# Expert tiles of 256 slots, with the inner layer turned and the first weight's parts fetched per tile

## The chip, the core and the metric

The kernel runs on one core of one Trainium2 chip. The metric is the device time of one execution in microseconds. The engines are named as in the profile: PE (matmul), PEld (its weight loads), DVE, ACT, POOL, SP, and 16 DMA engines that all queues share.

## What is computed

A graph network of two layers over 12,500 nodes and 200,000 edges is followed by a mixture of experts, to which the change belongs:

```python
logits = jnp.einsum('bsd,de->bse', xn, Wr) + br
top_vals, top_idx = jax.lax.top_k(logits, K)          # K = 2 of E = 8
w = jax.nn.softmax(top_vals, axis=-1)
...
for e in range(E):
    h = jax.nn.gelu(jnp.einsum('bsd,dh->bsh', xn, W1[e]) + b1[e], approximate=False)
    y_e = jnp.einsum('bsh,hd->bsd', h, W2[e]) + b2[e]
    y = y + y_e * w_full[..., e, None]
```

A row has D = 256 channels, the hidden layer H = 512, and the output 256. Everything is float32.

## The kernel before

The stages run one after the other with a barrier between them: the graph layers (`project_input`, `sum_layer`, `normalize_sums`, `project_hidden`, then the sums again), `route_tokens`, `list_tiles` and `run_experts`. The change is in the last two, and in `project_hidden`.

**project_hidden** takes the nodes in 24 chunks of 512 (and a last one of 256), two at a time. ACT normalizes (L1091), PE multiplies (L1111), DVE adds the bias (L1129), POOL takes the maximum with 0 (L1145), and SP stores 512 KB for each chunk (L1073). A buffer of `h` is written again only when its store from two chunks before has landed.

**route_tokens** writes one list of slots for each expert into the DRAM table `table`. Each entry has a token's row number and its weight. **list_tiles** counts the tiles of each expert on DVE, with one small step after the other, while SP loads all weights: `ffn_w1` and `ffn_w2` (4 MB each) and the biases, spread over all partitions.

**run_experts** goes over `FFN_TILES` = 204 tiles of 128 slots; a tile belongs to one expert, and a tile that no slot needs is run on dummy rows. First ACT and DVE split both weights into a high and a low part (16 pairs of instructions on 128x1024), since each product is made of three float32r products: high by high, high by low, low by high. For tile s the work is:

- POOL gathers its 128 rows from `tokens` (L1736, into one of `ROWS_HELD` = 6 places), 5 tiles ahead
- PE turns them (L1772, 2 transposes); ACT scales them by gamma and beta (L1854); DVE splits them (L1913, L1915)
- PE, first product: 6 matmuls of 512 columns (L1786); DVE adds b1 (L1906); ACT does gelu (L1860)
- PE turns the hidden rows (L1795, 4 transposes); ACT takes the high part (L1866), DVE the low one (L1922)
- PE, second product: 12 matmuls of 256 columns (L1804); DVE adds b2 (L1946); ACT weighs them by the slot's weight (L1885)
- POOL scatters the 128 result rows into `out`, adding to what is there (L1755)

The order on each engine is written out by hand, and every engine works through its own queue in order. PE's step s is: turn the rows of s+3, first product of s+2, turn the hidden rows of s+1, second product of s. POOL's step s is: gather s+5, then scatter s. SP loads the table (L1714) and holds back a scatter (L1725) until all scatters of the expert before have landed (`tile_after`), as two experts may add to one row. Tiles past the last used one all write to the same dummy rows, so each of them waits until the one before has landed.

## Time and profile before

| | |
|---|---|
| median of three runs | 5430.35 us (5423.59 to 5431.04) |
| the profiled execution | 5421.78 us |
| its span, first to last instruction | 5420.2 us |
| PE busy in the span | 4191.7 us (77%) |
| DVE busy | 3213.5 us (59%) |
| POOL busy | 3789.6 us (70%) |
| ACT busy | 966.8 us (18%) |
| DMA moved | 560.35 MB, mean 103 GB/s |

The span's busy shares are means over stages that have different limits. The graph sums fill most of the span and are not touched. `project_hidden` is a stretch of 103 us at 2155, and `run_experts` runs from 4580 us to the end, some 840 us. The profiled execution is 8.6 us shorter than the median of the runs.

### The profile page before, as it was taken

What the parts mean: (1) busy time and instruction counts of PE and PEld (TensorE: products, weight loads), DVE (VectorE), ACT (ScalarE), POOL (GpSimd) and SP (SyncE); (2) the same over time, 40 slices, a digit from 0 to 9 for tenths busy, and PEclk for the clock granted to TensorE, in tenths of its full rate; (3) what the DMA queues carried; (4) which work ended last, traced back from release to release, by engine and by line L of the source; (5) the groups of instructions that cost most, each with busy time, mean ns of one, the idle gap of its engine ahead of it and who ended that gap; (6) DMA issues with size and microseconds to landing.
All of it is one profiled execution on the core that took longest, in us unless ns stands there. A gap on an engine that the chain in (4) does not pass through costs nothing. (4 is left out here: it accounts for less than half of the span.)

```text
span 5420.2 us, 135489 instructions
## 1 busy us (share of the span) xinstructions
PE 4191.7 (77%) x20451; PEld 3507.4 (65%) x20452; DVE 3213.5 (59%) x9144; ACT 966.8 (18%) x2131; POOL 3789.6 (70%) x3818
## 2 busy tenths in 40 slices
PE   6778787778777874877878787777776672999998
PEld 5566666666666663766666666666665672888886
DVE  6555555555555556555555555555655664666665
ACT  3100000000000003200000000000001652566665
...
DMA packets 359801, 560.35 MB, mean 103 GB/s; under 512 B 128849, under 2 KB 253393, under 8 KB 359474
## 3 DMA queue, kind: packets, MB, share of 16 engines
...
q14 instruction: 48, 0.39, 0.0%
HBM read 479.80 MB, written 79.41 MB: 103 GB/s over the span
## 5 line engine op out<-in xcount | busy, mean ns | idle before, releaser
L788 POOL DMA_INDIRECT c_messages<-h,c_indices x3038 | 2879.9, 948 | 950.6 <-issue 918.3
L824 PE MATMUL c_partial<-c_onehot,c_messages 128*128 128x128 f32 x12544 | 2759.7, 371 | 851.2 <-DMA c_messages<-h,c_indices 448.0
L824 PEld LDWEIGHTS c_partial<-c_onehot,c_messages 128*128 128x128 f32 x12544 | 2263.1, 260 | 1350.4 <-issue 775.8
L867 DVE TENSOR_TENSOR sums<-sums,c_partial 128x256 f32 x3136 | 1321.0, 421 | 1590.0 <-PE c_partial L824 1531.5
L840 DVE TENSOR_SCALAR c_onehot<-iota,edge_dst,edge_w 128x128 f32<-128x128 f32 x3152 | 1148.2, 365 | 14.4 <-PEq L103 14.3
L750 ACT ACTIVATE c_indices<-edge_src 128x16 int32 (+1 forms) x200 | 42.9, 215 | 3706.6 <-PE c_partial L824 2752.9
L1755 POOL DMA_INDIRECT out<-ffn_result,ffn_table x204 | 326.4, 1600 | 213.9 <-ACT ffn_result L1885 127.4
L1736 POOL DMA_INDIRECT ffn_rows<-tokens,ffn_table x209 | 215.7, 1032 | 71.5 <-issue 57.2
L804 PE MATMUL c_z<-sums,w 128*128 x768 | 260.6, 501 | 0.0
L1398 POOL DMA_INDIRECT table<-rt_entry,rt_slot x196 | 203.8, 1040 | 69.2 <-issue 57.9
L1804 PE MATMUL ffn_ps<-ffn_w_high,ffn_hT_high 128*128 x816 | 246.9, 303 | 0.0
L1804 PE MATMUL ffn_ps<-ffn_w_high,ffn_hT_low 128*128 x816 | 229.6, 281 | 0.0
L1804 PE MATMUL ffn_ps<-ffn_w,ffn_hT_high 128*128 x816 | 229.5, 281 | 0.0
L804 PEld LDWEIGHTS c_z<-sums,w 128*128 128x128 f32 x768 | 198.4, 272 | 35.1
L1854 ACT ACTIVATE ffn_xT<-ffn_ps_x,beta,gamma 128x128 f32<-128x128 f32 x416 | 167.6, 453 | 178.6 <-PE ffn_ps_x L1772 177.1
L1913 DVE CAST ffn_xT_high<-ffn_xT 128x256 fp32r<-128x256 f32 x207 | 73.3, 354 | 192.6 <-ACT ffn_xT L1854 156.0
L1786 PE MATMUL ffn_ps<-ffn_w_high,ffn_xT_high 128*128 x412 | 183.8, 446 | 0.3 <-DVE ffn_xT_low L1915 0.3
L1922 DVE TENSOR_TENSOR ffn_hT_low<-ffn_ps_h,ffn_hT_high 128x512 fp32r<-128x512 f32 x205 | 141.7, 691 | 43.2 <-ACT ffn_hT_high L1866 39.5
L1786 PE MATMUL ffn_ps<-ffn_w_high,ffn_xT_low 128*128 x412 | 164.9, 400 | 0.0
L1786 PE MATMUL ffn_ps<-ffn_w,ffn_xT_high 128*128 x412 | 164.1, 398 | 0.0
L1772 PE MATMUL ffn_ps_x<-ident,ffn_rows 128*128 128x128 f32 x416 | 87.8, 293 | 89.4 <-DMA ffn_rows<-tokens,ffn_table 70.8
L1804 PEld LDWEIGHTS ffn_ps<-ffn_w,ffn_hT_high 128*128 128x128 f32 x816 | 154.7, 190 | 0.0
...
## 6 DMA issues: line engine op xcount, KB each, us to landing
...
```

What stands on the lines that cost most here:

```text
L788: pool.indirect_dma_start(messages[:, k, :], None, source, bass.IndirectOffsetOnAxis(ap=indices[:, k:k + 1], axis=0)).then_inc(s_message[k ...
L804: last = pe.matmul(z[:, co, :], t["w2"][:, k, co * P:(co + 1) * P], sums[:, k, bass.ds(chunk * Z_COLS, Z_COLS)], start=(k == 0), stop=(k = ...
L824: last = pe.matmul(partial[:, k % TURN_BANKS, g * P:(g + 1) * P], messages[:, k, g * P:(g + 1) * P], onehot[:, k % TURN_ONEHOTS, :], start ...
L840: return dve.tensor_scalar(onehot[:, slot, :], t["iota"][:], t["edge_dst"][:, bass.ds(step, 1)], t["edge_w"][:, bass.ds(step, 1)], ALU.is_ ...
L867: dve.tensor_tensor(where, where, partial[:, k % TURN_BANKS, 0:C].rearrange("p (g n) -> p g n", g=CG), ALU.add).then_inc(s_added, 1)
L1398: pool.indirect_dma_start(d["table"], bass.IndirectOffsetOnAxis(ap=slot[:, b, c, j:j + 1], axis=0), entry[:, b, c, j, :], None).then_inc(s ...
L1736: pool.indirect_dma_start(rows[:, row_slot, :], None, d["tokens"], bass.IndirectOffsetOnAxis(ap=table[:, k, 0:1], axis=0)).then_inc(s_rows ...
L1755: pool.indirect_dma_start(d["out"], bass.IndirectOffsetOnAxis(ap=table[:, k, 0:1], axis=0), result[:, k % 2, :], None, compute_op=ALU.add) ...
L1786: last = pe.matmul(ps_1[:, q, :], rows_part[:, q, g, :], w_part[:, bass.ds(e * (CG * HIDDEN) + g * HIDDEN, HIDDEN)], start=(g == 0 and n = ...
L1804: last = pe.matmul(ps_2[:, q, 0:C], rows_part[:, q, g * P:(g + 1) * P], w_part[:, bass.ds(e * (HG * C) + g * C, C)], start=(g == 0 and n = ...
L1854: act.activation(xT[:, q, g, :], ps_x[:, g * P:(g + 1) * P], ACT.Identity, bias=t["beta"][:, g:g + 1], scale=t["gamma"][:, g:g + 1]).then_ ...
L1922: dve.tensor_tensor(hT_low[:, q, :], ps_h[:, q, :], hT_high[:, q, :].bitcast(F32), ALU.subtract).then_inc(s_hT_low, 1)
```

## The change

- A tile has 256 slots (`TILE`), in two halves of 128, and there are (25088 + 8 * 255) // 256 = 105 tiles. POOL issues two gathers and two scatters for a tile, since each takes 128 rows.
- The first product is computed turned: the weight's 128x128 blocks are the stationary side and the 256 turned rows are the moving one, so that its result has the hidden channels on the partitions. It is now 24 matmuls of 256 columns. The transposes of the hidden rows are gone, b1 becomes a per-partition bias of gelu on ACT (from `b1T`), and both ACT steps write into PSUM in place. DVE takes both parts, in two halves of 128x512.
- The parts of the first weight don't stay on chip. `project_hidden` makes them, one expert with each of the first 8 pairs of chunks: it loads 512 KB, splits them on ACT and DVE, and stores 1 MB to the DRAM tensor `w1_parts`. `run_experts` fetches the 1 MB of the tile's expert for each tile on SP's queue (`load_parts`), into two buffers.
- `list_tiles` loads neither `ffn_w1` nor the spread b1; the split of 16 pieces at the start of `run_experts` is one of 8.
- The order by hand is a new one. PE's step s is: turn the rows of s+2, first product of s+1, second product of s. POOL's step s is: the two scatters of s, then the two gathers of s+4. `ROWS_HELD` is 4 tiles.

```diff
-FFN_TILES = PAIRS // P + EXPERTS
+TILE = 2 * P
+FFN_TILES = (PAIRS + EXPERTS * (TILE - 1)) // TILE
...
+            def load_expert(e):
+                gate(sp, s_part_low, e + 1, passed)
+                sp.dma_start(raw[:], d["w1"][bass.ds(e, 1), :, :].rearrange("o (k p) h -> p (o k) h", p=P)
+                             ).then_inc(s_raw, 16)
...
+            def store_parts(e):
+                gate(sp, s_part_low, e + 2, passed)
+                sp.dma_start(d["w1_parts"][bass.ds(e, 1), :, :].rearrange("o p w -> p (o w)"),
+                             parts[:].bitcast(F32).rearrange("p n k h -> p (n k h)")).then_inc(s_parts_stored, 16)
+
...
+            def split_high(e):
...
+                gate(act, s_raw, e * 16 + 16, passed)
+                gate(act, s_parts_stored, e * 16 + 16, passed)
+                act.activation(parts[:, 0, :, :], raw[:], ACT.Copy).then_inc(s_part_high, 1)
...
+            def split_low(e):
+                dve.wait_ge(s_part_high, e + 1)
+                dve.tensor_tensor(parts[:, 1, :, :], raw[:], parts[:, 0, :, :].bitcast(F32),
+                                  ALU.subtract).then_inc(s_part_low, 1)
...
-            sp.dma_start(t["ffn_b1"][:], d["b1"].rearrange("e h -> (e h)").partition_broadcast(P)).then_inc(biases, 16)
+            sp.dma_start(b1_rows[:], d["b1"].rearrange("e (k p) -> (e k) p", p=P)).then_inc(biases, 16)
             sp.dma_start(t["ffn_b2"][:], d["b2"].rearrange("e c -> (e c)").partition_broadcast(P)).then_inc(biases, 16)
             for e in range(E):
-                sp.dma_start(t["ffn_w1"][:, e * CG * HIDDEN:(e + 1) * CG * HIDDEN].rearrange("p (k h) -> p k h", k=CG),
-                             d["w1"][e].rearrange("(k p) h -> p k h", p=P)).then_inc(weights[e], 16)
                 sp.dma_start(t["ffn_w2"][:, e * HG * C:(e + 1) * HG * C].rearrange("p (k c) -> p k c", k=HG),
...
+            pe.transpose(b1T_ps[:, 0:E * HG], b1_rows[:], t["ident"][0:E * HG, 0:E * HG]).then_inc(s_b1T, 1)
...
-TABLES = 12
-ROWS_HELD = 6
-GATHER_AHEAD = 5
-TABLE_AHEAD = 8
+ROWS_HELD = 4
+TABLES = 8
+TABLE_AHEAD = 6
...
-        rows = sb("rows", [P, ROWS_HELD, C], F32)
+        rows = sb("rows", [P, ROWS_HELD, H, C], F32)
...
+            def load_parts(tile, q):
+                e = sp.value_load(t["tile_expert"][0:1, bass.ds(tile, 1)], min_val=0, max_val=E - 1)
+                sp.dma_start(w1_parts[:, q, :].bitcast(F32), d["w1_parts"][bass.ds(e, 1), :, :].rearrange("o p w -> p (o w)")
+                             ).then_inc(s_parts[q], 16)
 
...
+            def tile(i, s, k):
+                if not isinstance(s, int):
+
+                    gate(sp, s_one, s * 2 + 2, passed)
+                    load_parts(s + 2, k % 2)
+
+                for q in range(2):
+                    after = sp.value_load(t["tile_after"][0:1, q, bass.ds(s, 1)], min_val=16, max_val=AFTER_MAX)
+                    gate(sp, s_scatter[q], after, passed)
+                sp.sem_inc(s_turn, 1)
+                if not isinstance(s, int):
 
                     gate(sp, s_scatter[k % 2], landed(i, k), passed)
                     load(s + TABLE_AHEAD, (k + TABLE_AHEAD) % F)
+
...
-                pool.indirect_dma_start(rows[:, row_slot, :], None, d["tokens"],
-                                        bass.IndirectOffsetOnAxis(ap=table[:, k, 0:1], axis=0)
-                                        ).then_inc(s_rows[row_slot], 16)
+                for h in range(H):
+                    pool.indirect_dma_start(rows[:, row_slot, h, :], None, d["tokens"],
+                                            bass.IndirectOffsetOnAxis(ap=table[:, k, h, 0:1], axis=0)
+                                            ).then_inc(s_rows[row_slot], 16)
...
-            with pool.Fori(0, FFN_ROUNDS) as i:
-                for k in range(F):
-                    s = i * F + k
-                    ahead = k + GATHER_AHEAD
-
-                    gate(pool, s_xturn, s + GATHER_AHEAD + 1, passed)
+
+            def tile(i, s, k):
+
+                gate(pool, s_turn, s + 1, passed)
+                for h in range(H):
+                    gate(pool, s_result, s * H + (2 * H + h + 1), passed)
+                    pool.indirect_dma_start(d["out"], bass.IndirectOffsetOnAxis(ap=table[:, k, h, 0:1], axis=0),
+                                            result[:, k % 2, h, :], None, compute_op=ALU.add
+                                            ).then_inc(s_scatter[k % 2], 16)
+                if not isinstance(s, int):
+                    ahead = k + ROWS_HELD
+
+                    gate(pool, s_xturn, s + 1, passed)
                     gather(ahead % F, i + ahead // F, ahead % ROWS_HELD)
-                    gate(pool, s_turn, s + 1, passed)
-                    gate(pool, s_result, 2 + s + 1, passed)
-                    pool.indirect_dma_start(d["out"], bass.IndirectOffsetOnAxis(ap=table[:, k, 0:1], axis=0),
-                                            result[:, k % 2, :], None, compute_op=ALU.add
-                                            ).then_inc(s_scatter[k % 2], 16)
+            over_tiles(pool, tile)
...
-                    last = pe.transpose(ps_x[:, g * P:(g + 1) * P], rows[:, k % ROWS_HELD, g * P:(g + 1) * P],
-                                        t["ident"][:])
+                    for h in range(H):
+                        last = pe.transpose(ps_x[:, k % 2, g * TILE + h * P:g * TILE + (h + 1) * P],
+                                            rows[:, k % ROWS_HELD, h, g * P:(g + 1) * P], t["ident"][:])
                 last.then_inc(s_xturn, 1)
...
+                pe.wait_ge(s_parts[q], round_ * 16 + 16)
                 pe.wait_ge(s_xT_low, s + 1)
 
-                pe.wait_ge(s_pre, s + 1)
-                parts = ((xT_high, w1_high), (xT_high, w1_low), (xT_low, w1_high))
-                for g in range(CG):
-                    for n, (rows_part, w_part) in enumerate(parts):
-                        last = pe.matmul(ps_1[:, q, :], rows_part[:, q, g, :],
-                                         w_part[:, bass.ds(e * (CG * HIDDEN) + g * HIDDEN, HIDDEN)],
-                                         start=(g == 0 and n == 0), stop=(g == CG - 1 and n == 2))
-                last.then_inc(s_one, 1)
-            def turn_hidden(s, q):
-                pe.wait_ge(s_hidden, 2 + s + 1)
-
-                for g in range(HG):
-                    last = pe.transpose(ps_h[:, q, g * P:(g + 1) * P], hidden[:, q, g * P:(g + 1) * P], t["ident"][:])
-                last.then_inc(s_hturn, 1)
+                if not isinstance(s, int) or s > 1:
+                    pe.wait_ge(s_hT_low, s * 2)
+                parts = ((0, xT_high), (1, xT_high), (0, xT_low))
+                for hg in range(HG):
+                    for g in range(CG):
+                        for n, (w_part, rows_part) in enumerate(parts):
+                            last = pe.matmul(ps_1[:, q, hg, :],
+                                             w1_parts[:, q, ((w_part * CG + g) * HG + hg) * P:
+                                                      ((w_part * CG + g) * HG + hg + 1) * P],
+                                             rows_part[:, q, g * TILE:(g + 1) * TILE],
+                                             start=(g == 0 and n == 0), stop=(g == CG - 1 and n == 2))
+                    if hg % 2 == 1:
+                        last.then_inc(s_one, 1)
 
...
+                for h in range(H):
+                    for hg in range(HG):
+                        for n, (rows_part, w_part) in enumerate(parts):
+                            last = pe.matmul(ps_2[:, q, h, :], rows_part[:, q, hg, h * P:(h + 1) * P],
+                                             w_part[:, bass.ds(e * (HG * C) + hg * C, C)],
+                                             start=(hg == 0 and n == 0), stop=(hg == HG - 1 and n == 2))
                 last.then_inc(s_two, 1)
...
-            with pe.Fori(0, FFN_ROUNDS) as i:
-                for k in range(F):
-                    s = i * F + k
-                    if k == 0:
-                        experts = [expert_of(s + n) for n in range(3)]
-                    turn_rows(s + 3, k + 3, i * 2 + (k + 3) // ROWS_HELD)
-                    first_product(s + 2, k % 2, experts[2])
-                    turn_hidden(s + 1, (k + 1) % 2)
-                    second_product(s, k % 2, experts[0])
...
+            def tile(i, s, k):
+                e = expert_of(s)
+                if not isinstance(s, int):
+                    turn_rows(s + 2, k + 2, i * (F // ROWS_HELD) + (k + 2) // ROWS_HELD)
+                    first_product(s + 1, (k + 1) % 2, i * (F // 2) + (k + 1) // 2)
+                second_product(s, k % 2, e)
...
-                    act.activation(xT[:, q, g, :], ps_x[:, g * P:(g + 1) * P], ACT.Identity,
-                                   bias=t["beta"][:, g:g + 1], scale=t["gamma"][:, g:g + 1]).then_inc(s_xT, 1)
+                    here = ps_x[:, q, g * TILE:(g + 1) * TILE]
+                    act.activation(here, here, ACT.Identity, bias=t["beta"][:, g:g + 1],
+                                   scale=t["gamma"][:, g:g + 1]).then_inc(s_xT, 1)
...
-                act.wait_ge(s_pre, 2 + s + 1)
-                act.activation(hidden[:, q, :], pre[:, q, :], ACT.Gelu).then_inc(s_hidden, 1)
-                act.activation(hT_high[:, q, :], ps_h[:, q, :], ACT.Copy).then_inc(s_hT, 1)
+                e = act.value_load(t["tile_expert"][0:1, bass.ds(s, 1)], min_val=0, max_val=E - 1)
+                for hg in range(HG):
+                    if hg % 2 == 0:
+                        act.wait_ge(s_one, s * 2 + (hg // 2 + 1))
+                    act.activation(ps_1[:, q, hg, :], ps_1[:, q, hg, :], ACT.Gelu,
+                                   bias=b1T[:, bass.ds(e * HG + hg, 1)]).then_inc(s_hidden, 1)
...
+                for h in range(H):
+                    act.activation(result[:, k % 2, h, :], yb[:, k % 2, h, :], ACT.Copy,
+                                   scale=table[:, k, h, 1:2].bitcast(F32)).then_inc(s_result, 1)
...
+            def tile(i, s, k):
+                if not isinstance(s, int):
+                    scale_rows(s + 2, k % 2)
+                    activate(s + 1, (k + 1) % 2)
+                weigh(i, s, k)
...
-                dve.tensor_copy(xT_high[:, q, :, :], xT[:, q, :, :]).then_inc(s_xT_high, 1)
+                dve.tensor_copy(xT_high[:, q, :], ps_x[:, q, :]).then_inc(s_xT_high, 1)
...
+                for half in range(2):
+                    a, b = half * 2, half * 2 + 2
+                    dve.wait_ge(s_hidden, s * HG + b)
...
+                    dve.tensor_copy(hT_high[:, q, a:b, :], ps_1[:, q, a:b, :]).then_inc(s_hT_high, 1)
+                    dve.wait_ge(s_hT_high, s * 2 + half + 1)
+                    dve.tensor_tensor(hT_low[:, q, a:b, :], ps_1[:, q, a:b, :], hT_high[:, q, a:b, :].bitcast(F32),
+                                      ALU.subtract).then_inc(s_hT_low, 1)
...
+                dve.tensor_tensor(yb[:, q, :, :], ps_2[:, q, :, :],
+                                  b2[:, bass.ds(e * C, C)].unsqueeze(1).to_broadcast([P, H, C]),
+                                  ALU.add).then_inc(s_yb, 1)
...
+            def tile(i, s, k):
+                if not isinstance(s, int):
+                    split_rows(s + 2, k % 2)
+                    split_hidden(s + 1, (k + 1) % 2)
+                bias_two(s, k % 2)
```

On POOL, the start of its list in the experts and the first steps of the loop. Before; `ffn_rows` are gathers, `out` scatters:

```order
L1742 DMA ffn_primer<-in_src 128x2 x2
L1736 DMA ffn_rows<-tokens,ffn_table 128x256 x5
L1745 UNCONDITIONAL_BRANCH
L1745 ISA
L85 ISA
L1736 DMA ffn_rows<-tokens,ffn_table 128x256
L85 REGISTER_ALU x2
L1755 DMA out<-ffn_result,ffn_table 12672x256
```

and after:

```order
L1805 DMA ffn_primer<-in_src 128x2 x2
L1799 DMA ffn_rows<-tokens,ffn_table 128x256 x8
L1747 UNCONDITIONAL_BRANCH
L1747 ISA
L86 ISA
L1814 DMA out<-ffn_result,ffn_table 12800x256
L86 REGISTER_ALU
L1814 DMA out<-ffn_result,ffn_table 12800x256
L86 ISA
L1799 DMA ffn_rows<-tokens,ffn_table 128x256 x2
```

The gather of a step stood ahead of its scatter, and now both gathers stand behind both scatters of the step.

On PE, one step of the loop. Before (the block of three matmuls on L1804 repeats three more times):

```order
L1772 MATMUL ffn_ps_x<-ident,ffn_rows 128x128 x2
...
L1786 MATMUL ffn_ps_1<-ffn_w1_high,ffn_xT_high 128x512
...
L1786 MATMUL ffn_ps_1<-ffn_w1,ffn_xT_high 128x512
L1786 MATMUL ffn_ps_1<-ffn_w1_high,ffn_xT_low 128x512
...
L1795 MATMUL ffn_ps_h<-ident,ffn_hidden 128x128 x4
...
L1804 MATMUL ffn_ps_2<-ffn_w2_high,ffn_hT_high 128x256
```
and after (the pair of rows on L1856 repeats to 24 matmuls, the three on L1871 to 24):

```order
L1839 MATMUL ffn_ps_x<-ident,ffn_rows 128x128 x4
...
L1856 MATMUL ffn_ps_1<-ffn_xT_high,ffn_w1_parts 128x256 x2
L1856 MATMUL ffn_ps_1<-ffn_xT_low,ffn_w1_parts 128x256
...
L1871 MATMUL ffn_ps_2<-ffn_w2_high,ffn_hT_high 128x256
...
L1871 MATMUL ffn_ps_2<-ffn_w2,ffn_hT_high 128x256
L1871 MATMUL ffn_ps_2<-ffn_w2_high,ffn_hT_low 128x256
```

The transposes of the hidden rows are gone, all matmuls have 256 columns, and a step of PE has one tile between the second product of a tile and the turn of the rows four tiles on, where there were two steps between second product and the turn of the rows that POOL gathered behind its scatter.

## Rows read from the trace of the kernel before

**Rows 1.** The page's first line.

```profile
span 5420.2 us, 135489 instructions
```

**Rows 2.** Windows, the loop: us; busy PE, PEld, DVE, ACT, POOL; PEclk; DMA; GB/s.

```profile
4620.00:5385.00 765.00, 729.57 (x4794) 638.76 (x4793) 500.36 (x999) 467.05 (x999) 514.13 (x398) 1.00 0.43 69
```

**Rows 3.** Groups by line, 4650 to 5380: form, count | busy us, mean ns | idle before.

```profile
L1755 POOL DMA_INDIRECT out<-ffn_result,ffn_table x191 | 305.6, 1600 | 179.2 <-ACT ffn_result L1885 107.0 <-issue 55.8 <-SPq L1725 8.6
...
L1922 DVE TENSOR_TENSOR ffn_hT_low<-ffn_ps_h,ffn_hT_high 128x512 fp32r<-128x512 f32 x191 | 132.0, 691 | 38.9 <-ACT ffn_hT_high L1866 35.2 <-issue 0.8
```

**Rows 4.** The chain of waits around 5000 to 5035: start us, us, what.

```profile
5001.98 3.78 DMA out<-ffn_result,ffn_table
...
5024.27 3.05 DMA ffn_rows<-tokens,ffn_table
...
5027.44 0.43 PE ffn_ps_x L1772 x2
5027.87 1.45 PE ffn_ps L1786 x6
5029.33 0.44 PE ffn_ps_h L1795 x4
5029.76 1.42 PE ffn_ps L1804 x12
```

**Rows 5.** Timeline, 5000 to 5005: start us, us, instruction [idle before].

```profile
5000.65 0.50 ACT L1885 ACTIVATE ffn_result<-ffn_yb,ffn_table 128x256 f32<-128x256 f32 x1
...
5001.98 1.60 POOL L1755 DMA_INDIRECT out<-ffn_result,ffn_table  x1 [0.97 <-ACT ffn_result L1885]
...
5002.95 0.28 PE L1804 MATMUL ffn_ps<-ffn_w_high,ffn_hT_low 128*128 x1
...
5003.38 0.42 DVE L1946 TENSOR_TENSOR ffn_yb<-ffn_ps,ffn_b 128x256 f32<-128x256 f32 x1 [0.21 <-PE ffn_ps L1804]
...
5003.89 0.98 POOL L1736 DMA_INDIRECT ffn_rows<-tokens,ffn_table  x1 [0.31 <-issue]
...
5004.19 0.50 ACT L1885 ACTIVATE ffn_result<-ffn_yb,ffn_table 128x256 f32<-128x256 f32 x1
```

**Rows 6.** Waits, 4650 to 5380: us in total, times, longest.

```profile
PE ffn_ps_x L1772 <- DMA ffn_rows<-tokens,ffn_table: 17.8, 27, 1.9
```

**Rows 7.** Windows at the loop's start, as in Rows 2.

```profile
4609.00:4612.50 3.50, 1.55 (x9) 0.94 (x7) 1.28 (x3) 1.32 (x3) 0.00 (x0) 0.98 0.00 0
4612.50:4619.40 6.90, 5.42 (x20) 4.74 (x21) 2.89 (x6) 3.03 (x6) 0.00 (x0) 0.51 0.00 0
4619.40:4626.00 6.60, 6.60 (x46) 5.97 (x46) 4.07 (x10) 3.80 (x9) 2.64 (x2) 1.00 0.18 21
```

**Rows 8.** Timeline of PE at the loop's start.

```profile
4613.98 0.69 PE L1772 MATMUL ffn_ps_x<-ident,ffn_rows 128*128 128x128 f32 x2 [2.02 <-issue]
```

**Rows 9.** Windows: 20 us in which the weights were loaded.

```profile
4560.00:4580.00 20.00, 0.00 (x0) 0.00 (x0) 12.85 (x42) 0.22 (x1) 0.00 (x0) 0.50 1.04 375
```

**Rows 10.** Timeline of the experts' start.

```profile
4574.02 0.26 DVE L1643 TENSOR_SCALAR tile_after<-lt_after_i 1x212 int32<-1x212 int32 x1
...
4578.18 0.71 SPq L1592 DMA_DIRECT2D ffn_w<-in_w  x1
...
4580.64 13.78 SPq L1714 DMA_DIRECT2D ffn_table<-table  x10
...
4580.86 18.25 DVE L1894 TENSOR_TENSOR ffn_w<-ffn_w,ffn_w_high 128x1024 fp32r<-128x1024 f32 x16 [6.58 <-ACT ffn_w_high L1841]
```

**Rows 11.** Timeline of POOL: the span's last scatters.

```profile
5401.65 1.59 POOL L1755 DMA_INDIRECT out<-ffn_result,ffn_table  x1 [1.90 <-SPq L1725]
...
5407.26 1.59 POOL L1755 DMA_INDIRECT out<-ffn_result,ffn_table  x1 [2.73 <-SPq L1725]
```

**Rows 12.** Groups by line in project_hidden, 2155 to 2259.

```profile
L1145 POOL TENSOR_SCALAR ph_h<-ph_biased 128x256 f32<-128x256 f32 x98 | 90.6, 950 | 13.9 <-DVE ph_biased L1129 13.9
...
L1129 DVE TENSOR_TENSOR ph_biased<-ph_product,ph_b 128x256 f32<-128x256 f32 x98 | 35.8, 417 | 49.2 <-DMA h<-ph_h 34.2 <-PE ph_product L1111 15.0
```

253 lines of the change are left out of this document (114 added, 139 removed).

## The prediction

> **What bounds the kernel now.** I read the windows by stage first, then the groups by line in the experts, the chain of waits there, and the timeline of two tiles. The span is 5420.2 us [rows 1], and `run_experts` starts at 4580.6, where SP loads the first table [rows 10]. In its loop PE is busy 729.6 of 765 us at a granted clock of 1.00, while POOL is busy 514 and the DMA engines 43% [rows 2]. So PE is the bound there. The chain shows what one tile of 128 slots costs on PE: 0.43 (turn) + 1.45 (first product, 6 matmuls of 512 columns) + 0.44 (turn of hidden) + 1.42 us (second product, 12 of 256) = 3.74 us [rows 4]. The spacing in the groups' window is 730 / 191 = 3.82 us [rows 3], and 204 tiles take 779 us.
>
> The second thing to see is how near the gather is. POOL's gather for s+5 is issued after the scatter of s-1. From the end of a second product: 0.15 us to DVE's bias (5002.95 + 0.28 to 5003.38), 0.42 for it, 0.39 until ACT starts, 0.50 for ACT [rows 5], 0.83 until POOL starts (5000.65 + 0.50 to 5001.98), 1.60 for the scatter and 0.31 of gap [rows 5], and 3.17 from the gather's start to the turn that used it (5024.27 to 5027.44) [rows 4]. That is 7.37 us, against two steps of PE, 7.48. It just fits, and PE waited for a gather 27 times, for 17.8 us in all [rows 6].
>
> **The change, part by part.**
>
> *PE's work.* A tile of 256 slots needs 4 transposes (0.44, as the four of hidden), 24 matmuls of 256 columns for the first product and 24 for the second. 12 such take 1.42 us [rows 4], so 0.44 + 2.84 + 2.84 = 6.12 us for 256 slots, where it was 7.48. If PE stayed the bound, 105 tiles would take 643 us, 136 less. From the turn's start to the end of the last matmul I take 6.3, since the last one's 0.28 reaches 0.16 past its slot.
>
> *The loop through POOL.* Now POOL's step is two scatters of s and then two gathers of s+4, and PE's step s+2 begins with the turn of s+4. Between the end of the second product of s and that turn there is but one step of PE (6.1 us). The path is: 0.15 + 0.69 (the bias on 128x512, as L1922 [rows 3]) + 0.39 + 0.50 (ACT's first half) + 0.83 + 2 x 1.91 (scatters) + 1.29 (first gather, 0.98 + 0.31) + 3.17 (second gather, to the turn) = 10.84 us, from [rows 4, 5]. PE is in order: the turn that waits holds back the first product of s+3 and the second product of s+2, which feed the next scatter. So two tiles take 10.84 + 6.3 = 17.1 us or 8.57 each, where the same 256 slots took 7.64. The larger tile costs POOL no less per slot, and the order costs a step of cover. This is what I expect to decide.
>
> *The clock.* PE would work 12.3 us for two tiles and then stand idle. The even and the odd tiles start one right after the other at the loop's head, and nothing parts them later, as the odd tile's turn is ready before the even one's step is over; so the idle time comes in one piece, about 4.7 us. In the trace PE was mostly idle from 4609.9 to 4614.0 [rows 8]; the clock went from 0.98 to 0.51, and was back at 1.00 only 5.4 us after PE had resumed [rows 7]. These are the levels of 2.4 and 1.2 GHz, so 5.4 us of slow work lose 2.7 us. The bounds are 0 (gaps of up to 1.9 us in the loop [rows 6] left the clock at 1.00 [rows 2]) and 2.7 us for each pair. I take 2.2, near the row with the like gap. The Trainium skill (TensorE: Matmul & The Clock Gate, "HAM oscillation — how this bites in real kernels") tells of a loop whose wait for a DMA throttles PE so that each tile starts cold; it speaks against this change, and the trace agrees at the one place where there is such a gap.
>
> *The fetch of 1 MB for each tile.* While the weights were loaded the DMA engines moved 375 GB/s [rows 9], so 1 MB takes 2.8 us. The buffer is free two steps ahead, when the first product of s is done, so the fetch itself is hidden (over 10 us of cover), and the engines are busy 43% of 7.6 us + 2.8 = 6.1 us of a period over 8. But it shares them with the gathers. Bounds: 0 (they don't meet) and 2.8 us for each pair (all of it lies ahead of the gather that PE waits for). It is issued about 1 us after a first product, and most of it is over when the gathers run, so I take 0.3. The skill (DMA: Bandwidth & Descriptors, "Queues, rings and completion order") says that each engine takes turns between the queues with work. By that rule a fetch in flight delays a gather by its own share; no row here shows it.
>
> *DVE and ACT.* DVE has three casts and three subtractions of 128x512 and a bias: 7 x 0.69 [rows 3] = 4.8 us; ACT 8 steps of 256 at 0.50 [rows 5] = 4.0; POOL 3.82 + 2.58 = 6.4. All lie beside a period of over 8 us.
>
> Together: two tiles take 17.1 + 2.2 + 0.3 = 19.6, one 9.82.
>
> *The head.* `list_tiles` ended with SP's loads (4578.2 + 0.7), and DVE had finished at 4574.3 [rows 10]. With half the loads DVE's chain ends it, on a list of 113 in place of 212, some 3 us earlier: 7.5 us gained. The splits are 8 instead of 16, at 18.25 / 16 = 1.14 each [rows 10], so DVE is through at about 4582.5. Then turn, scale, split (3.7 us), first product in part at the low clock (5), one step of turn, first and second product (6.2): the first second product ends at 4597.5, give or take 5.
>
> *The tail.* From the end of the last but one second product: 4.5 to its second scatter, 3.8 to land [rows 4], 1.8 through SP to the next scatter (5401.65 + 3.8 to 5407.26 [rows 11]), since the dummy tiles go one by one, 1.9 + 3.8 for that, and 9.1 from the last landing to the end (5407.26 + 3.8 to 5420.2): 24.8 us.
>
> *project_hidden.* 8 pairs of chunks get a load of 0.5 MB and a store of 1 MB on SP's queue, the one of the stores for which DVE already waits 34.2 us in 25 chunks; POOL is busy 90.6 of 103 us, so the stage has little slack [rows 12]. 1.5 MB at 375 GB/s [rows 9] is 4.2 us. Bounds are 0 and 8 x 4.2 = 33; ACT's and DVE's splits (1 us each) fit beside POOL. I take 14, as only one of a pair's two stores comes behind it.
>
> **Sum.** 4597.5 + 103 x 9.82 + 24.8 + 14 = 5648 us of span against 5420: +228 us. The profiled execution's span stands 10 us below the median of the runs; with that kept, 5430 + 228 = **5658 us**.
>
> **Rivals.**
>
> *The clock holds.* Nothing but the 1.9 us gaps speaks for it, and noise that evens out the spacing. Then 8.57 a tile: 4597.5 + 882.7 + 24.8 + 14 = 5519, or 5529 as median. Chance 0.25.
>
> *The fetches hit the gathers in full.* 10.84 + 6.3 + 2.8 + 2.2 = 22.1, 11.07 a tile: 5777 of span, 5787. For it speaks that the DMA engines are over 70% busy; against it the order in time. Chance 0.12.
>
> *Faster: the gathers don't bind.* If the gather reached PE within 8.1 us of the second product instead of 10.8 (POOL's waits shorter than 0.83, a scatter that overlaps the next), the next bound would be the ring of DVE and ACT, which wait for each other in their written order: bias 0.69, hop 0.39, weigh 1.0, scale 1.0, hops 0.1, then rows' and hidden's splits 6 x 0.67 = 4.0, so 7.2 us a tile. 4597.5 + 741.6 + 24.8 + 14 = 5378, or 5388. It decides if two gathers and two scatters take under 5.5 us from POOL's first start to the turn, where the rows give 8.3. Chance 0.09.
>
> **How the numbers follow.** My forecast has 0.50, the held clock 0.25, the hit gathers 0.12, the ring 0.09; 0.02 is left for about no change and 0.02 for slower in another way. The first two span 5515 (head and project_hidden at their low ends) to 5730 (a pair at 20.9), and the range is that; what it leaves out is the ring, most of the hit gathers and the rest, about 0.2. A difference of 0.2% is what a measurement of this kernel can tell from no change: faster 0.09, same 0.02, slower 0.89.
>
> **What would show it.** Right, if PE's longest wait in the loop is on the turn of the rows for the gather, near 4 us every second tile, if the distance of tiles is 9.3 to 10.3 us and the granted clock in the loop is clearly below 1 (near 0.85). The held clock is shown by 1.00 and 8.6 us. If gathers take well over 3.2 us to land, the fetch is to blame. If PE waits for `hT_low`, or DVE for ACT, with the gathers long landed, the ring is the bound and I am wrong. project_hidden should be 103 + 14 us.

## The result, and the profile after

The kernel became slower: 5699.7 us (median; 5697.2 to 5702.5), beside 5427.0 for the kernel before in the same runs. The ratio is 1.0502, with a 95% interval from 1.0486 to 1.0518. The forecast was 5658, with a range of 5515 to 5730. The profiled execution has a span of 5695.7 us, 275.5 more than [rows 1]; 228 were forecast.

First the page's own line, then the windows (us; busy PE, PEld, DVE, ACT, POOL; PEclk; DMA; GB/s): the loop, three stretches of one pair of tiles, and `project_hidden`.

```profile
span 5695.7 us, 131791 instructions
```

```profile
4640.00:5600.00 960.00, 685.04 (x4911) 674.60 (x4912) 446.81 (x659) 323.47 (x756) 488.33 (x378) 0.84 0.61 155
5006.00:5012.00 6.00, 0.57 (x5) 0.36 (x3) 1.98 (x4) 0.91 (x2) 4.24 (x5) 0.85 0.78 232
5012.00:5017.00 5.00, 4.65 (x22) 4.65 (x23) 1.39 (x2) 1.80 (x4) 3.14 (x3) 0.50 0.66 102
5017.00:5021.00 4.00, 4.00 (x36) 4.00 (x36) 2.80 (x5) 0.81 (x2) 0.00 (x0) 1.00 0.27 68
2158.00:2290.00 132.00, 97.57 (x392) 81.85 (x392) 63.83 (x131) 44.68 (x58) 93.01 (x98) 0.85 0.58 193
```

Beside [rows 2] the loop's story is in one line: PE was busy 95% at full clock, and is now busy 71% at 0.84. The three short stretches show how: 6 us in which PE hardly works, 5 us of work at the level of 1.2 GHz (0.50), and then 2.4 GHz again. The DMA engines went from 43 to 61%.

What PE waits for, 4650 to 5600 (us in total, times, longest), answers to [rows 6], where it was 17.8 us:

```profile
POOL out L1814 <- ACT ffn_result L1923: 384.8, 94, 8.4
PE ffn_ps_x L1839 <- DMA ffn_rows<-tokens,ffn_table: 271.5, 50, 7.4
```

POOL itself waits for results, so it isn't what bounds. PE has one wait for a gather for about every second tile, so the tiles run in pairs. The chain of one pair (start us, us, what) answers to [rows 4]:

```profile
5000.56 0.70 DVE ffn_yb L1978
...
5001.36 0.52 ACT ffn_result L1923
...
5002.71 0.57 POOL out L1814
...
5006.52 1.01 POOL ffn_rows L1799
5007.53 0.30 issue
5007.84 4.47 DMA ffn_rows<-tokens,ffn_table
...
5012.35 1.12 PE ffn_ps_x L1839 x4
5013.47 4.47 PE ffn_ps L1856 x24
5017.94 2.89 PE ffn_ps L1871 x24
...
5020.97 0.70 DVE ffn_yb L1978
```

It is the path of the forecast: second product, bias, weighing, two scatters, two gathers, turn, and PE's own order to the next second product. Two terms are to be seen in it. The gather takes 4.47 us to land, 3.80 in the next pair, where it was 3.05 [rows 4]. And PE takes 8.48 us from the turn to the last matmul (1.12 + 4.47 + 2.89), where 6.3 is its time at full clock.

The distances of two biases, DVE's timeline (start, us, instruction, idle before), show the pairs: 7.1, 13.1, 7.3 and 10.8 us.

```profile
5020.97 0.69 DVE L1978 TENSOR_TENSOR ffn_yb<-ffn_ps,ffn_b 128x512 f32<-128x512 f32 x1 [0.63 <-PE ffn_ps L1871]
5028.08 0.69 DVE L1978 TENSOR_TENSOR ffn_yb<-ffn_ps,ffn_b 128x512 f32<-128x512 f32 x1 [0.34 <-issue]
5041.13 0.69 DVE L1978 TENSOR_TENSOR ffn_yb<-ffn_ps,ffn_b 128x512 f32<-128x512 f32 x1 [0.69 <-PE ffn_ps L1871]
5048.41 0.69 DVE L1978 TENSOR_TENSOR ffn_yb<-ffn_ps,ffn_b 128x512 f32<-128x512 f32 x1 [0.50 <-issue]
5059.18 0.69 DVE L1978 TENSOR_TENSOR ffn_yb<-ffn_ps,ffn_b 128x512 f32<-128x512 f32 x1 [0.60 <-PE ffn_ps L1871]
```

From the first bias (4632.6) to the last but one (5677.1) there are 103 distances, 10.14 us each.

`project_hidden`, 2158 to 2290, answers to [rows 12]. The stage took 129.9 us where it took 99.2 by the same first and last instruction:

```profile
ACT ph_parts L1126 <- DMA ph_raw<-in_w: 52.3, 8, 9.5
DVE ph_biased L1163 <- PE ph_product L1145: 46.2, 48, 8.7
```

ACT, which works in order, waits for the raw weight eight times ahead of a split, and DVE, which used to wait for the stores of `h`, now waits for PE and through it for ACT.

### The profile page after: what moved, and what is told of

It reads as the page before. It is cut to its first block and busy times, and to the rows that moved or that the text cites. A ratio compares the mean times of both kernels' runs of the same rounds, so it can differ in the third digit from the quotient of the medians.

```text
span 5695.7 us, 131791 instructions
## 1 busy us (share of the span) xinstructions
PE 4206.4 (74%) x20996; PEld 3601.6 (63%) x20997; DVE 3189.5 (56%) x8853; ACT 845.1 (15%) x1943; POOL 3801.4 (67%) x3831
## 5 line engine op out<-in xcount | busy, mean ns | idle before, releaser
L1856 PE MATMUL ffn_ps<-ffn_xT_high,ffn_w_parts 128*128 128x256 f32 x1680 | 392.8, 334 | 0.0
L1856 PEld LDWEIGHTS ffn_ps<-ffn_xT_high,ffn_w_parts 128*128 128x128 f32 x1680 | 329.9, 240 | 0.0
L1956 DVE CAST ffn_xT_high<-ffn_ps_x 128x512 fp32r<-128x512 f32 x106 | 73.3, 692 | 431.0 <-ACT ffn_ps_x L1907 429.0
L1839 PEld LDWEIGHTS ffn_ps_x<-ident,ffn_rows 128*128 128x128 f32 x424 | 62.7, 179 | 337.6 <-DMA ffn_rows<-tokens,ffn_table 304.4
L1856 PE MATMUL ffn_ps<-ffn_xT_low,ffn_w_parts 128*128 128x256 f32 x840 | 271.6, 323 | 0.0
L1871 PE MATMUL ffn_ps<-ffn_w_high,ffn_hT_low 128*128 x840 | 237.7, 283 | 0.0
L1871 PE MATMUL ffn_ps<-ffn_w_high,ffn_hT_high 128*128 x840 | 237.7, 283 | 0.0
L1871 PE MATMUL ffn_ps<-ffn_w,ffn_hT_high 128*128 x840 | 236.0, 281 | 0.0
L1856 PEld LDWEIGHTS ffn_ps<-ffn_xT_low,ffn_w_parts 128*128 128x128 f32 x840 | 197.4, 235 | 0.0
L1915 ACT ACTIVATE ffn_ps<-ffn_ps,ffn_b1T 128x256 f32<-128x256 f32 x420 | 169.0, 444 | 144.6 <-PE ffn_ps L1856 143.3
```

The source lines that it names most:

```text
L1839: last = pe.transpose(ps_x[:, k % 2, g * TILE + h * P:g * TILE + (h + 1) * P], rows[:, k % ROWS_HELD, h, g * P:(g + 1) * P], t["ident"][:])
L1856: last = pe.matmul(ps_1[:, q, hg, :], w1_parts[:, q, ((w_part * CG + g) * HG + hg) * P: ((w_part * CG + g) * HG + hg + 1) * P], rows_part[ ...
L1871: last = pe.matmul(ps_2[:, q, h, :], rows_part[:, q, hg, h * P:(h + 1) * P], w_part[:, bass.ds(e * (HG * C) + hg * C, C)], start=(hg == 0 ...
L1915: act.activation(ps_1[:, q, hg, :], ps_1[:, q, hg, :], ACT.Gelu, bias=b1T[:, bass.ds(e * HG + hg, 1)]).then_inc(s_hidden, 1)
```

## The experiments

In this section "after" is the changed kernel. For the loop I took three numbers out of each trace, as means over the turns of rows for which PE stood idle over 1 us: **landing** is the time from the start of a tile's second gather on POOL to the turn that uses it; **bias to turn** from DVE's bias of tile s to the turn of s+4; **turn to bias** from there to the bias of that PE step. The last two add up to a pair. **Experts** is the time from the hand-over by `list_tiles` (in the changed kernels DVE's copy into `b1T`) to the end of POOL's last scatter.

| kernel | landing | bias to turn | turn to bias | us per tile | clock in the loop | experts, us |
|---|---|---|---|---|---|---|
| after (e5: 4.77, 11.97, 8.28) | 4.71 | 11.96 | 8.33 | 10.14 | 0.84 | 1086.6 |
| e2, no fetch | 2.82 | 10.12 | 8.58 | 9.32 | 0.87 | 1003.6 |
| e3, filled even tiles | 5.31 | 12.50 | 7.91 | 10.19 | 0.875 | 1094.5 |
| e6, filled both | 5.67 | 12.86 | 7.37 | 10.11 | 0.95 | 1085.2 |
| e9, filled, no fetch | no waits | no waits | no waits | 8.55 | 1.00 | 926.1 |
| e1, gathers first | | | | 7.41 | 0.97 | 807.2 |
| e8, three orders | | | | 7.23 | 0.96 | 790.9 |
| e11, and the table | | | | 7.16 | 0.97 | 782.1 |
| e12, few fetches | | | | 6.54 | 0.99 | 719.9 |

The kernel before took 829.1 us in the experts. The runs e1 to e4 and e9 to e11 were on chips where each of the two graph sums took some 3400 us instead of 1910, the kernel before 8381 and 8440 us in all. So totals are compared only with the kernel before on the same chip, and mechanisms by the stages that took their usual time there: `project_hidden` in e4, which has that of the kernel before, took 98.8 us, and the experts of e10, whose loop is that of after, 1091.2. The experts of e7, which have that loop too, took 1093.0, so some 6 us in this column are no difference.

**The order on POOL (e1).** The theory: the loss is the order, scatters ahead of gathers. The rival: the larger tile and its fetch.

```diff
             def tile(i, s, k):
+                if not isinstance(s, int):
+                    ahead = k + ROWS_HELD
+                    gate(pool, s_xturn, s + 1, passed)
+                    gather(ahead % F, i + ahead // F, ahead % ROWS_HELD)
                 gate(pool, s_turn, s + 1, passed)
                 for h in range(H):
...
-                if not isinstance(s, int):
-                    ahead = k + ROWS_HELD
-                    gate(pool, s_xturn, s + 1, passed)
-                    gather(ahead % F, i + ahead // F, ahead % ROWS_HELD)
```

> The changed kernel with one thing moved: POOL's two gathers of s+4 stand ahead of the two scatters of s, as the gather did before. Theory (POOL's written order decides): the gathers of s+4 then wait for the second product of s-1 only, two PE steps ahead, so PE stops waiting for them; the next bound is PE (6.3) or the ring of DVE and ACT (7.2), 7.0 to 7.5 us a tile where 10.14 was measured, and the granted clock goes back to near 1.00. 103 x 2.8 = 290 us less than the changed kernel: about 5410 (5380 to 5450). Rival (the 1 MB fetches hold the gathers up): the gathers land as late as now, PE still waits for them, over 5600.

Measured: 8366.0 us beside 8380.9, ratio 0.9979 (0.9968 to 0.9990). The loop, 7600 to 8300:

```profile
7600.00:8300.00 700.00, 613.22 (x4899) 598.67 (x4898) 438.78 (x659) 309.50 (x756) 489.09 (x377) 0.97 0.82 212
```

```profile
ACT ffn_result L1923 <- DVE ffn_yb L1978: 306.5, 82, 4.1
...
PE ffn_ps_x L1839 <- DMA ffn_rows<-tokens,ffn_table: 49.1, 45, 2.9
```

The same instructions in another order take 279 us less in the experts. A tile takes 7.41 us, PE's wait for gathers falls from 271.5 in 950 us to 49.1 in 700, and the clock comes back by itself, to 0.97. So the order was the cause of the loss. With the order of before, the experts gain 22 us by the change (807.2 for 829.1), which `project_hidden` takes away again: as a whole, e1 is within 0.3% of the kernel before.

**The same order in the kernel before (e4).** If the order alone is to blame, the kernel before must suffer from it too.

```diff
-                    gate(pool, s_xturn, s + GATHER_AHEAD + 1, passed)
-                    gather(ahead % F, i + ahead // F, ahead % ROWS_HELD)
                     gate(pool, s_turn, s + 1, passed)
...
+                    gate(pool, s_xturn, s + GATHER_AHEAD + 1, passed)
+                    gather(ahead % F, i + ahead // F, ahead % ROWS_HELD)
```

> The kernel before with one thing moved: POOL's scatter of s stands ahead of the gather of s+5. Theory: between a second product and the turn that its scatter holds up lies one PE step of 3.74 us instead of two, against a path of 7.37; two tiles of 128 take 11.1 us instead of 7.64, so 203 x 1.74 = 353 us more, 5780, and up to 200 more if the clock falls in the gaps: 5750 to 6000. Rival (the order is harmless and the larger tile or the fetch is the cause): under 5480.

Measured: 9120.6 us, ratio 1.0878 (1.0842 to 1.0913); 7.41 us for 128 slots where it was 3.84. The direction was right and the size was not. Its chain, 7800 to 7816:

```profile
7798.75 2.75 DMA ffn_rows<-tokens,ffn_table
...
7801.63 0.45 PE ffn_ps_x L1772 x2
...
7802.46 0.45 ACT ffn_xT L1854
7802.91 0.41 ACT ffn_result L1885
...
7804.14 0.51 POOL out L1752
...
7806.04 2.79 DMA ffn_rows<-tokens,ffn_table
```

The expectation had two steps of PE in the circle. But ACT is in order as well: it scales the newly turned rows ahead of weighing the result for which POOL's scatter waits. So the circle is gather, turn, scale, weigh, scatter, gather, with one tile in it. In the kernel before the gather stands ahead of that scatter, which opens the circle; exchanging the two calls cost 740 us.

**The fetch (e2).** Nothing is fetched in the loop; the first product works with the parts of the first two tiles.

```diff
-                    gate(sp, s_one, s * 2 + 2, passed)
-                    load_parts(s + 2, k % 2)
...
-                pe.wait_ge(s_parts[q], round_ * 16 + 16)
+                pe.wait_ge(s_parts[q], 16)
...
```

> The changed kernel without the fetch of the first weight's parts for tiles 2 to 104: only the two fetches at the start are left, so the first product of every tile uses the parts of the first tiles' expert, and the output differs from the reference's. Theory: the fetch is hidden and only lengthens a gather by some 0.5 us of the path of 11.35, once in two tiles: 25 to 60 us less than 5700, so 5640 to 5675, PE still waits for the gathers. Rival (contention is the cause): the path falls by 2.8 us or more and the time by 150 us or more, under 5560.

Measured: 8559.5 us, ratio 1.0209 (1.0184 to 1.0233). The experts take 83 us less than after, more than the 25 to 60 of the theory and well short of the 150 of the rival. The landing falls from 4.71 to 2.82 us and is nearly the same each time (longest 2.95, where it was up to 6.25). So the fetch delays the gather that PE waits for by 1.9 us a pair, where I had put 0.3.

**The clock (e3, e6, e9).** 24 matmuls whose result is overwritten, ahead of the turn of even tiles. They write where the turn will, so the wait for that place to be free goes ahead with them:

```diff
+                if not isinstance(s, int) or s > 1:
+
+                    pe.wait_ge(s_xT_low, s - 1)
+                    if k % 2 == 0:
+                        for n in range(24):
+                            pe.matmul(ps_x[:, k % 2, 0:C], w2_high[:, 0:P], w2_high[:, 0:C], start=True, stop=True)
                 pe.wait_ge(s_rows[k % ROWS_HELD], round_ * (16 * H) + 16 * H)
-                if not isinstance(s, int) or s > 1:
-
-                    pe.wait_ge(s_xT_low, s - 1)
```

> The changed kernel with 24 extra matmuls of 256 columns (2.9 us at the high clock) ahead of PE's wait for the gather of every even tile, where it stands idle for about 5 us; their output is overwritten. Theory (the low clock after each gap costs some 2.2 us of each pair): the granted clock goes to 0.97 or more, two tiles take 11.35 + 6.3 = 17.7 us instead of 20.3, and the time is 5550 to 5600. Rival (the low clock is hidden, or costs nothing on the path): within 20 us of 5700, or slower.

Measured: 8644.3 us, ratio 1.0305 (1.0280 to 1.0331); the experts took 8 us more than after, hardly more than e7 and e10 with the loop of after. For most of the loop the waiting tiles were the odd ones, so the filling ran between the two tiles of a pair, and a gap of 3.6 us remained, with a clock of 0.875. So e6 has 20 of them ahead of every turn (the `if` is left out), and e5 is the changed kernel itself beside it.

> The changed kernel itself, so that the other kernels of this group have it on their own chip. All theories: the loop's mean distance of tiles is 10.1 us with pairs of some 13.4 and 7.1 us and a granted clock of 0.84; project_hidden takes 130 us; some 5700 us in all if the graph sums take what they took in the first profile.

> Ahead of every turn of rows PE runs 20 extra matmuls of 256 columns (2.4 us at full clock) whose result is overwritten. A pair of tiles leaves PE idle for some 5.8 us, so the 4.8 us of them fit into the idle time, and 1 us of it stays. Theory: the low clock costs 2.2 us of each pair, on the path. Then the loop's granted clock rises to 0.95 or more, turn, first and second product of the tile that waited take 6.3 us and not 8.5, a pair takes 11.35 + 6.3 = 17.7 us, a tile 8.8 to 9.1, and the kernel 105 to 135 us less than the changed one. Rival: the low clock lies beside the gathers and costs nothing; then the time doesn't change by more than 10 us although the clock is high. A second way to miss: the first attempt of this kind (24 matmuls ahead of the even tiles alone) put them into the step that didn't wait and left a gap of 3.4 us, at 0.875; if the clock stays below 0.9 here too, the run says nothing on its price.

Measured: e5 5703.3 us, ratio 1.0521 (1.0503 to 1.0538); e6 5683.5, ratio 1.0477 (1.0460 to 1.0495). So the clock went to 0.95 and only 20 us came of it, in the medians. The table goes by the profiled executions, and those of e5 and e6 both took 5696 us. As the rival would have it? The chain says otherwise:

```profile
5012.20 1.01 POOL ffn_rows L1799
...
5013.52 5.93 DMA ffn_rows<-tokens,ffn_table
...
5019.50 0.66 PE ffn_ps_x L1841 x4
```

Turn to bias is 0.96 us shorter than after (7.37 for 8.33), but the landing is 0.96 longer (5.67 for 4.71). The first is half of the clock's price: in 20 of the 49 pairs the step after the wait took 6.5 us, in the other 29 the clock fell again and it took 8.0. The second comes from the place of the fetch, which SP issues behind a first product. After a pair's first tile, the filling stands ahead of the next first product as well and delays it by its own 2.4 us, so the fetch is issued 0.8 us ahead of the second gather (5012.75 here, for 5013.52) where it is some 3.3 us ahead in after. So the edit itself moved the fetch onto the gathers, and that took the gain. If so, there is nothing to take where nothing is fetched: e9 has both edits.

> Both edits together: 20 overwritten matmuls ahead of each turn keep PE busy, and the first product uses the parts fetched for the first two tiles, so that nothing is fetched in the loop (its products are not the reference's). With the filling alone a waiting turn stood 5.67 us behind the start of its second gather, without the fetch alone 2.82, with neither 4.71. Theory: the filling did save PE's time of a pair, and the gather that ran further into the fetch gave it back. Without a fetch there is nothing to give back: bias to turn 10.1 us, turn to bias 6.5 to 6.9, a pair 16.6 to 17.0, a tile 8.3 to 8.5 where it was 9.32 without the fetch alone, and some 85 to 105 us less than that in the experts. Rival: the clock's low time isn't on the path; then a tile stays at 9.1 to 9.4 us.

Measured: 8549.2 us, ratio 1.0126 (1.0109 to 1.0143). The window 7700 to 8500:

```profile
7700.00:8500.00 800.00, 799.97 (x6739) 799.69 (x6738) 437.56 (x654) 330.22 (x748) 484.89 (x374) 1.00 0.40 62
```

PE is busy throughout at 1.00, and a tile takes 8.55 us, 0.77 less than without the fetch alone; 77.5 us less in the experts. Now PE and its filling are the bound (6.1 + 2.4 us a tile), so the low clock cost at least that much there. The idle time costs the clock, and the clock is on the path.

**project_hidden (e7, e10).** First, SP loads the next expert ahead of the store of the parts:

```diff
-            over_chunks(sp, store, load_expert, store_parts)
+            load_expert(0)
+            with sp.Fori(0, EXPERTS - 1) as i:
+                for u in range(U):
+                    store(i, i * U + u, u, TILES)
+                load_expert(i + 1)
+                store_parts(i)
...
```

> In project_hidden alone: SP issues the next expert's load of 512 KB ahead of the 1 MB store of the expert before, not behind it. Theory: the stage's 30.6 extra us came from ACT, which works in order and waited 52 us for the raw weight, because its load stood behind the store on SP's queue. Then the stage takes 103 to 113 us where it took 130, ACT's wait for the raw weight falls below 15 us, and the kernel is 17 to 27 us faster than the changed one. Rival: the 1.5 MB of each pair take DMA time that the stage hasn't got, 4.2 us for each of the eight; the stage stays above 122 us.

Measured: 5698.9 us, ratio 1.0506 (1.0488 to 1.0524), beside 5703.3 for e5: nothing to speak of. The stage took 130.6 us. Its waits, 2158 to 2290:

```profile
ACT ph_parts L1138 <- DMA w_parts<-ph_parts: 52.8, 7, 9.5
```

The same 53 us, with another name. The split waits for two things, its raw weight and the landing of the last store out of the one buffer of parts; I had moved one out of the way and found the other. So e10 has two buffers of parts too:

```diff
-        parts = sb("parts", [P, 2, CG, HIDDEN], F32R)
+        parts = sb("parts", [P, 2, 2, CG, HIDDEN], F32R)
...
```

> In project_hidden alone: the load ahead of the store, as before, and now two buffers of split parts, so that ACT's split waits for the store of the expert before the last, not of the last. With the load alone moved, ACT waited the same 53 us, for the landing of the 1 MB store out of the one buffer. Theory: the 30 us are the round trip of one buffer, store behind two stores of h on one queue, then split, and ACT in order ahead of the next chunk. With two the stage takes 103 to 115 us where it took 130, and ACT's wait at the split is below 15 us in all; the kernel is 15 to 27 us faster than the changed one. Rival: the queue itself is full (2.5 MB for each pair of chunks); then DVE and POOL wait for the stores of h instead and the stage stays above 122 us.

Measured: 8708.3 us, ratio 1.0318 (1.0301 to 1.0335); the stage took 119.9 us, 10 less, and not the 15 to 27 of the theory:

```profile
ACT ph_parts L1144 <- DMA ph_raw<-in_w: 43.8, 8, 7.9
```

ACT still comes first: by the written order SP reaches the load only when POOL has finished the second chunk of the pair, and ACT works ahead of POOL. e12 puts this to the test.

**Toward a better version (e8, e11, e12).** e8 is e1 and e7, and on ACT the scaling of s+3 stands ahead of the weighing of s (the start of ACT's list and the end of PE's follow it):

```diff
             def tile(i, s, k):
                 if not isinstance(s, int):
-                    scale_rows(s + 2, k % 2)
                     activate(s + 1, (k + 1) % 2)
+                    scale_rows(s + 3, (k + 1) % 2)
                 weigh(i, s, k)
...
```

> The changed kernel with three orders exchanged: POOL's gathers of s+4 ahead of the scatters of s; the load ahead of the store in project_hidden; and on ACT the scaling of the rows of s+3 ahead of the weighing of s, which opens the ring DVE bias, ACT weigh, ACT scale, DVE split. With the gathers first alone a tile took 7.41 us. Theory: the ring was what bounded it then; POOL's two gathers and two scatters, 2 x 1.29 + 2 x 1.91 = 6.4 us, are next, and PE's 6.12 us just below. A tile takes 6.4 to 6.9 us, the granted clock in the loop is 0.97 or more, and the kernel takes 5700 - 280 (gathers) - 20 (load) - 0.5 to 1.0 x 103 (ring) = 5300 to 5350 us, or 350 to 400 us less than the changed kernel on the same chip. Rival: the gathers' landing beside the fetches, not the ring, set the 7.41; then a tile stays at 7.3 to 7.5 us and the kernel takes about 5400.

Measured: 5397.9 us, ratio 0.9961 (0.9947 to 0.9975), 7.23 us a tile. That is the rival's time, and nearly its tile of 7.3 to 7.5. In 4640 to 5360 DMA was at 84%, and PE waited for the fetch itself:

```profile
PE ffn_ps L1868 <- DMA ffn_w_parts<-w_parts: 34.1, 11, 5.2
```

e11 has e10's buffers, and SP waits for the scatters of s-3 before it loads a table, no longer of s-2 (except in one tile of eight):

```diff
-TABLE_AHEAD = 6
+TABLE_AHEAD = 5
...
-                    gate(sp, s_scatter[k % 2], landed(i, k), passed)
+                    if k == 0:
+                        gate(sp, s_scatter[0], landed(i, 0), passed)
+                    else:
+                        gate(sp, s_scatter[(k + 1) % 2], landed(i, k - 1), passed)
```

> The version with the three orders exchanged, which took 5398 us beside 5421 of the kernel before, with two buffers of parts in project_hidden and the table's load on SP waiting for the scatters of s-3 where it waited for those of s-2. In that version SP, in order, came to the fetch of 1 MB up to 5 us late behind that wait, and PE waited 34 us in 690 for the fetch. Theory: with both, project_hidden takes 103 to 115 us (20 less), a tile 6.7 to 7.0 us (7.23 before), and the kernel 5325 to 5360 us, 0.982 to 0.988 of the kernel before. Rival: the fetch and the gathers fill the DMA engines (84% busy) and set the 7.2 us whatever the order of SP; then only project_hidden's 20 us are gained and it takes 5378 or so.

Measured: 8400.6 us, ratio 0.9953 (0.9937 to 0.9970), and 7.16 us a tile. `project_hidden` took 119.8 us, as in e10. Again the rival: SP's order hardly mattered, and PE still waited 38 us for the fetch. Twice the order of a queue was not what held the loop; what remained to try was the fetch's amount. e12 fetches only for a new expert, and loads the raw weights two experts ahead into two buffers:

```diff
-                    load_parts(s + 2, k % 2)
+                    new = sp.value_load(t["tile_expert"][0:1, bass.ds(s + 2, 1)], min_val=0, max_val=E - 1)
+                    old = sp.value_load(t["tile_expert"][0:1, bass.ds(s, 1)], min_val=0, max_val=E - 1)
+                    with sp.If(new != old):
+                        sp.dma_start(w1_parts[:, k % 2, :].bitcast(F32),
+                                     d["w1_parts"][bass.ds(new, 1), :, :].rearrange("o p w -> p (o w)")
+                                     ).then_inc(s_parts[k % 2], 16)
+                    with sp.Else():
+                        sp.sem_inc(s_parts[k % 2], 16)
```

> The version with the orders exchanged, with two changes more. SP fetches the 1 MB only where the expert of tile s+2 isn't that of tile s, so that most tiles fetch nothing, and the result is the same. In project_hidden there are two buffers of raw weight too, loaded two experts ahead. Theory on the loop: once the order is right, the fetch is what holds a tile at 7.2 us, by PE's waits for it (38 us in 643) and by the gathers it delays; without most fetches a tile takes 6.4 to 6.7 us, set by PE's 6.12 and POOL's 6.4, DMA share falls from 84% to about 45%, and the experts take 55 to 80 us less than in the version before (782 us). Theory on project_hidden: ACT's wait at the split came from the load's place behind stores on SP's queue that run up to two chunks later than ACT; with the load a pair earlier the wait falls below 10 us (44 before) and the stage from 120 to 102 to 110 us. Rivals: the ring between DVE and ACT holds the tile at 7.1 whatever is fetched; the stores' traffic holds the stage at 118 or more. In all 0.975 to 0.985 of the kernel before, by theory, where its graph sums take what they took in the first profile.

Measured: 5309.0 us (5305.7 to 5311.9) beside 5421.3, ratio 0.9792 (0.9775 to 0.9808). It beats both kernels. The window of its loop, and POOL's timeline:

```profile
4640.00:5270.00 630.00, 607.00 (x4988) 596.63 (x4987) 455.08 (x672) 320.70 (x768) 496.66 (x384) 0.99 0.57 104
```

```profile
5006.26 1.01 POOL L1829 DMA_INDIRECT ffn_rows<-tokens,ffn_table  x1 [0.30 <-ACT ffn_result L1955]
5007.58 0.98 POOL L1829 DMA_INDIRECT ffn_rows<-tokens,ffn_table  x1 [0.30 <-issue]
5008.86 1.63 POOL L1849 DMA_INDIRECT out<-ffn_result,ffn_table  x1 [0.30 <-issue]
5010.79 1.58 POOL L1849 DMA_INDIRECT out<-ffn_result,ffn_table  x1 [0.30 <-issue]
5012.67 1.01 POOL L1829 DMA_INDIRECT ffn_rows<-tokens,ffn_table  x1 [0.30 <-ACT ffn_result L1955]
```

14 fetches are left in that window. POOL issues without a pause, 6.41 us from one tile's first gather to the next (5006.26 to 5012.67), but for 15 gaps that make 17 us of the 630; it is the bound now, with PE just below. A tile takes 6.54 us, the experts 719.9, and 62 us less than e11 is what the fetch cost there. The DMA share fell from 86 to 57%, not to the 45 expected. `project_hidden` took 112.7 us, a little over the 102 to 110 expected: ACT's wait at the splits is down to 13 us (12.0 for the store, 1.0 for the load), and DVE waits 35.7 us for the stores of `h`, as in [rows 12]. e12 changed two things at once. They lie in stages with a barrier between, so each is read from its own stage.

## Why the prediction was right, and where its sizes were off

**The order decides: right, and shown.** The forecast put the loss on the circle scatter, gather, turn, and e1 takes 279 us away by that order alone. The circle with its waits stands in the chain as it was written.

**Pairs: right.** 7.1 us and 13 us, one idle piece for each pair, as the argument on bunching said. Which half of the tiles waits may change on the way: the 10.8 us above is such a place, while in e2 the even tiles waited throughout.

**The path, by its terms.** Forecast from bias to turn: 10.84 - 0.15 + 0.3 = 10.99; measured 11.96. Up to the second gather it is 7.25, where the sum had 7.52, since the two waits on ACT and POOL were somewhat shorter. The gather with its landing was 3.17 in the sum and is 2.82 with nothing beside it (e2). These two together gave back 0.6.

**The fetch beside the gathers: the failed size.** The step "most of it is over when the gathers run, so I take 0.3" was wrong. 4.71 - 2.82 = 1.9 us a pair, inside the bounds of 0 and 2.8 but far from the value taken. The forecast's argument from order in time had used the lone 375 GB/s of [rows 9], at which 1 MB takes 2.8 us. In the trace of after, SP issues the fetch some 3.3 us ahead of the second gather in most pairs, and the packets of a fetch begin 1.1 us after its issue and end 5.4 us after it (mean of 101 fetches; 4.3 to 7.7). So most fetches are still under way when both gathers start. The pair at 5012 shows it (POOL's, SP's and PE's lines; the turn is 4.51 us behind the gather):

```profile
5004.59 0.33 SPq L1765 DMA_DIRECT2D ffn_w_parts<-w_parts  x1
...
5007.84 0.98 POOL L1799 DMA_INDIRECT ffn_rows<-tokens,ffn_table  x1 [0.30 <-issue]
...
5012.35 1.12 PE L1839 MATMUL ffn_ps_x<-ident,ffn_rows 128*128 128x128 f32 x4 [5.79 <-DMA ffn_rows<-tokens,ffn_table]
```

The same trace has five waited gathers for which no fetch was issued from 9 us before the gather to the turn. They landed within 2.74 to 2.85 us, and all others took 3.48 us or more. One of the five is followed by a tile whose second gather has the fetch issued behind it, and is slow all the same (turns 2.74 and 5.35 us behind their gathers):

```profile
5048.43 0.98 POOL L1799 DMA_INDIRECT ffn_rows<-tokens,ffn_table  x1 [0.30 <-issue]
...
5051.17 1.11 PE L1839 MATMUL ffn_ps_x<-ident,ffn_rows 128*128 128x128 f32 x4 [4.17 <-DMA ffn_rows<-tokens,ffn_table]
...
5051.97 0.33 SPq L1765 DMA_DIRECT2D ffn_w_parts<-w_parts  x1
...
5055.75 0.98 POOL L1799 DMA_INDIRECT ffn_rows<-tokens,ffn_table  x1 [0.30 <-issue]
...
5057.09 0.33 SPq L1765 DMA_DIRECT2D ffn_w_parts<-w_parts  x1
...
5061.10 0.92 PE L1839 MATMUL ffn_ps_x<-ident,ffn_rows 128*128 128x128 f32 x4 [2.07 <-DMA ffn_rows<-tokens,ffn_table]
```

The Trainium skill's rule (DMA: Bandwidth & Descriptors, "Queues, rings and completion order") that an engine takes turns between the queues with work fits what is seen: fetches issued ahead of a gather and behind it both lie in its time. The forecast had named the rule and had no row for it; e2 and e6 are such rows (2.82 without a fetch, 5.67 where it is issued 0.8 us ahead). That the engines are shared is shown by them; in what turns they are shared isn't.

**The clock: right in kind, a little large in size.** 2.2 us was taken. Measured: 8.33 us turn to bias, where it is 6.45 at full clock by the sum (6.5 in the 20 turns of e6 after which the clock held), so 1.9. Idle, then 0.50, then 1.00 is in the windows above. That the term lies on the path is shown by e9. e6 alone doesn't show it, as its filling gave back on the landing what it took off the clock's term.

**The pair and the loop.** 11.96 + 8.33 = 20.3 us against 19.64: +0.97 on the way to the turn and -0.32 on PE. One tile 10.14 against 9.82, and 103 of them +33 us.

**project_hidden: mis-sized.** 30.7 us for 14. The failed step is "ACT's and DVE's splits (1 us each) fit beside POOL", together with a price by bandwidth alone. The splits' own time fits; their place doesn't. ACT is in order, and a split that waits for a load or a store on SP's queue holds back the next chunk. e7 and e10 show the wait moving from the load to the store and back, and with both a pair ahead (e12) the stage is 13.5 us longer than before, which is what the 14 had priced. That it agrees so well is partly luck: the upper bound, 33 us, came from traffic, and nearly all of it was reached by another cause.

**The head.** The first second product ended at 4632.4, where the sum had 4597.5 + 14. `project_hidden` gives 16.7 of the 20.9. `list_tiles` took 7.5 us less, as forecast. The rest is about 4: the first turn came 1.2 us later than the sum had it, and 3 are at the second turn, which waited 5.12 us for its gather, since POOL's first three gathers took 1.9 us each; that wait wasn't in the sum.

**The tail.** 18.6 us from the last but one bias to the end (5677.1 to 5695.7), and 24.8 were forecast. What was too long is the end: 12.9 us from the start of the last scatter (5407.26 [rows 11]) to the end before, and 7.9 now (5687.79). Why the end is shorter by 5 us I didn't find out.

**The sum.** +20.9 (head) + 33 (loop) - 6.2 (tail) = +47.7, on a forecast of +228, which is the 275.5 measured but for rounding.

**The rivals.** The held clock fell (0.84). That the fetches hit the gathers in full fell too, but it was nearer to the truth than the 0.3 taken: 1.9 of its 2.8 us. The ring was not to be seen as long as the gathers bound. With gathers first a tile took 7.41, near its 7.2, and ACT waited 306.5 of 700 us for DVE's bias; but opening the ring (e8) gave 0.2 us only, and cutting the fetch 0.6. So its number was met by something else, for the larger part: by the fetch, as e12 shows.
